# Recommender tower on one core: lookup groups of 8 to 10 blocks in a ring of 17, and gram products in runs of 64 samples

## What is computed

```python
    e = jnp.stack([tbl_0[ids[:, 0]], tbl_1[ids[:, 1]],
...
    gram = jnp.einsum('bfd,bgd->bfg', all_emb, all_emb)
    return gram[:, _TRIU_I, _TRIU_J]
...
    h = jnp.concatenate([z, r_bottom_output], axis=1)
    h = jnp.maximum(h @ W_top1 + b_top1, 0.0)
    h = jnp.maximum(h @ W_top2 + b_top2, 0.0)
    y = h @ W_top3
```

## Time and profile before

| | us |
|---|---|
| median of 3 runs (358.92 to 360.71) | 360.54 |
| span of the profiled execution | 357.7 |
| PE busy in it | 334.8 (94%) |
| DVE busy | 267.5 (75%) |
| POOL busy | 254.7 (71%) |
| ACT busy | 205.6 (57%) |

### The profile page before, as it was taken

One profiled execution on the slowest core, in us unless ns is written; L12 is line 12 of the kernel. 1 busy time (PEld: TensorE's weight loads), 2 busy tenths in 40 slices (PEclk: granted clock), 3 DMA queues, 4 the chain that ended last, 5 costly groups with the idle time before them and its releaser, 6 DMA issues.

```text
span 357.7 us, 14104 instructions
## 1 busy us (share of the span) xinstructions
PE 334.8 (94%) x6020; PEld 295.8 (83%) x6020; DVE 267.5 (75%) x810; ACT 205.6 (57%) x336; POOL 254.7 (71%) x274
## 2 busy tenths in 40 slices
PE   0678989899999999999999999999999999999996
PEld 0677889798988988888888888889888888888885
DVE  1999999994868869598777978788696987732412
ACT  3585776232334774757757566849666578552232
POOL 4777777777777777777777777777777777777600
DMA  6657468332225855849567496657766394732200
GB/s 211 180 166 244 136 172 295 96 83 63 55 53 112 150 113 106 131 101 176 101 129 131 84 151 134 127 104 121 155 99 141 85 175 109 106 83 57 58 5 1
DMA packets 60013, 42.91 MB, mean 120 GB/s; under 512 B 48816, under 2 KB 51504, under 8 KB 59824
## 3 DMA queue, kind: packets, MB, share of 16 engines
q1 hardware_dynamic: 51216, 24.38, 33.2%
q0 software_dynamic: 8448, 17.32, 20.9%
q10 hardware_dynamic: 288, 0.33, 0.4%
HBM read 31.24 MB, written 0.01 MB: 87 GB/s over the span
## 4 chain that ended last, share of the span: by engine, by line
PE 53%; DVE 16%; POOL 12%; DMA 9%; issue 5%; ACT 2%; SPq 2%; ACTq 0%; DVEq 0%
PE hot_ps L458 18%; POOL X L406 12%; DVE onehot L682 11%; PE h_ps L490 8%; PE gram_ps L436 8%; PE xt_ps L458 7%; PE h_ps L535 5%; DMA ids_wide<-in_hot_ids_dram 4%; PE h_ps L487 3%; DVE tab L749 2%; DMA stage_sb<-in_hot_dram 2%; DMA X<-in_table_dram,rows_sb 2%; PE xt_ps L420 1%; DMA turned<-planes 1%; PE zt_ps L472 1%
## 5 line engine op out<-in xcount | busy, mean ns | idle before, releaser
L406 POOL DMA_INDIRECT X<-in_table_dram,rows_sb x264 | 253.3, 959 | 83.3 <-issue 78.9
L682 DVE TENSOR_SCALAR onehot<-ids_wide,row_value 128x256 fp32r<-128x256 int16 x665 | 206.2, 380 | 39.2 <-PE hot_ps L458 23.2
L458 PE MATMUL hot_ps<-onehot,tab 128*128 128x256 f32 x1072 | 149.5, 291 | 14.4 <-ACT tab L861 11.1
L458 PEld LDWEIGHTS hot_ps<-onehot,tab 128*128 128x128 f32 x1072 | 135.2, 193 | 17.8 <-issue 15.3
L658 ACT COPY XT<-turned 128x512 int16<-128x512 int16 x82 | 65.7, 883 | 8.6 <-DMA turned<-planes 8.6
L832 ACT COPY XT<-hot_ps 128x256 f32<-128x256 f32 x60 | 41.2, 686 | 50.4 <-PE hot_ps L458 50.2
L436 PEld LDWEIGHTS gram_ps<-XT 128*27 128x27 f32 x4096 | 40.6, 105 | 28.3 <-issue 18.1
L436 PE MATMUL gram_ps<-XT 128*27 128x26 f32 x4096 | 53.0, 190 | 4.4 <-DVE Z L690 3.3
L822 ACT COPY planes<-X 128x1024 int16<-128x1024 int16 x41 | 44.5, 1086 | 13.2 <-DMA X<-in_table_dram,rows_sb 13.2
L490 PE MATMUL h_ps<-stage_sb,w_sb 128*128 128x256 f32 (+3 forms) x192 | 44.2, 366 | 0.0
L458 PE MATMUL xt_ps<-onehot,tab 128*128 128x256 f32 x288 | 40.8, 288 | 0.0
(11 more groups left out here) (54 smaller groups left out, 134.9 us busy)
## 6 DMA issues: line engine op xcount, KB each, us to landing
ids_wide<-in_hot_ids_dram SPq DMA_DIRECT2D x14, 320.0 KB, 4.6
X<-in_table_dram,rows_sb POOLq DMA_INDIRECT x264
stage_sb<-in_hot_dram SPq DMA_DIRECT2D x15, 256.0 KB
stage_sb<-in_hot_dram SPq DMA_DIRECT2D x10, 192.0 KB
bottomT<-in_bottom_t_dram SPq DMA_DIRECT2D x8, 128.0 KB
w_sb<-in_w_dram SPq DMA_DIRECT2D x1, 1024.0 KB
turned<-planes SPq DMA_TRANSPOSE x41
w_sb<-in_w_dram SPq DMA_DIRECT2D x1, 512.0 KB, 9.3
```

The costliest lines, as they stand in the source:

```text
L406: pool.indirect_dma_start(X[:, n % RING, k, :], None, table, bass.IndirectOffsetOnAxis(idx[:, column:column + 1], 0)).then_inc(gathered[n ...
L458: mm = pe.matmul(hot_bank(i)[:, 0:WIDE], tab[u][:, part, D * c:D * (c + 1)], onehot[p % ONEHOTS][:, c - PIECE[u][h], :], start=(c == 0 and ...
L682: compared = dve.tensor_scalar(onehot[p % ONEHOTS][:, c - PIECE[u][h], :], ids_wide[:, u, :], row_value[:, c:c + 1], None, ALU.is_equal)
```

## The change

**Groups.** The 64 blocks are cut into seven groups of 8, 9, 9, 10, 9, 10 and 9 blocks (`TAKEN`) instead of eight of 8. A lookup product has 32 columns for each block of its group, so 256, 288 or 320; each group after the first still has 180 products. The slices spread them over the blocks of the group before: 22 or 23 a block in blocks 0 to 7, 20 in groups of 9 blocks, 18 in groups of 10. No lookups are left from block 55 on.

**Ring.** XT is a ring of 17 blocks instead of 16, indexed by block. A copy that crosses the end of the ring is made as two (`kept`): all placings of groups 3 and 5 and some copies of outside vectors. Since a group may be longer than what is free, ScalarE holds back the placings of a group's first blocks until enough of the ring is free (`placed_in`), and places them together in the first block where it is.

**One-hots.** Pieces are now two chunks (`BITE`), in six buffers: 12 chunks instead of 20 places. Loading and splitting of the tables stays in pieces of up to 4 chunks (now 4 + 4 + 2 for 10).

**Order of tables.** From group 2 on (the third group) the tables are looked up in reverse, the five of 10 chunks first.

**Order on TensorE.** From block 16 to 53 (`TURN_FROM` to `LAST` - 2) two blocks are one step, `half_tile`: the lookups of both, the gram products of both, then the MLP steps of both.

The rest follows from these: narrower slices of the id lists, the waits of the lists by group, and the scratch of ScalarE's share of the comparisons, which moves into a buffer of the DMA transposes.

```diff
-XTILES = 4
-WIDE = 2 * P
+KEPT = 17
-ONEHOTS = 5
+ONEHOTS = 6
+BITE = 2
-GROUPS = TILES // 2
+TAKEN = [8, 9, 9, 10, 9, 10, 9]
+GROUPS = len(TAKEN)
+STARTS = [sum(TAKEN[:n]) for n in range(GROUPS + 1)]
+WIDE = PAD * max(TAKEN)
...
+ORDER = [list(range(HOTS[n])) if n < 2 else list(range(HOT))[::-1] for n in range(GROUPS)]
...
+        def placed_in(b):
+
+            early = STARTS[GROUP_OF[b] + 2] - KEPT if GROUP_OF[b] + 2 <= GROUPS else 0
+            if b < early:
+                return []
+            if b == early:
+                return [i for k in range(STARTS[GROUP_OF[b]], b + 1) for i in ended(k)]
+            return ended(b)
...
-                    mm = pe.matmul(hot_bank(i)[:, 0:WIDE], tab[u][:, part, D * c:D * (c + 1)],
-                                   onehot[p % ONEHOTS][:, c - PIECE[u][h], :],
+                    mm = pe.matmul(hot_bank(i)[:, 0:width(n)], tab[u][:, part, D * c:D * (c + 1)],
+                                   onehot[p % ONEHOTS][:, c - BITES[u][h], 0:width(n)],
...
+            def half_tile(b):
+
+                t, j = b // BLOCKS, b % BLOCKS
+                lookups(*slice_of(b))
+                lookups(*slice_of(b + 1))
+                gram(b)
+                gram(b + 1)
+                mlp(t, j)
+                mlp(t, j + 1)
...
-            for b in range(LAST - 1):
+            for b in range(TURN_FROM):
                 step(b)
+            for b in range(TURN_FROM, LAST - 2, 2):
+                half_tile(b)
+            step(LAST - 2)
             last_blocks()
...
-                wait(act, gram_full, 2 * BLOCKS * (n - 1))
-                act.copy(XT[:, at:at + 2, :, hot_slot(u)], hot_bank(i)[:, 0:WIDE].rearrange("d (t s) -> d t s", t=2)
-                         ).then_inc(hot_placed, 1)
+                wait(act, gram_full, STARTS[n + 1] - KEPT)
+                for begin, end, at in kept(STARTS[n], STARTS[n + 1]):
+                    columns = slice(PAD * (begin - STARTS[n]), PAD * (end - STARTS[n]))
+                    placed = act.copy(XT[:, at, :, hot_slot(u)],
+                                      hot_bank(i)[:, columns].rearrange("d (b s) -> d b s", s=PAD))
+                placed.then_inc(hot_placed, 1)
...
-                for i in ended(b)[:1]:
+                placed = placed_in(b)
+                for i in placed[:1]:
                     place_hot(i)
                 split_words(UNITS_OF.get(b + AHEAD, []))
                 for p in pieces_ended(b):
                     one_hot_share(p + ONEHOTS)
-                for i in ended(b)[1:]:
+                for i in placed[1:]:
                     place_hot(i)
```

More of the change, by code:

```diff
@@ L72, in hot_slot, with pieces, kept @@
     return BOTTOM_SLOT + 1 + u if u < HOT_BASE else ALWAYS + u - HOT_BASE
-def pieces(chunks):
-    count = -(-chunks // PIECE_MAX)
-    return [-(-chunks * h // count) for h in range(count + 1)]
+def pieces(chunks, most):
+    return list(range(0, chunks, most)) + [chunks]
+def kept(begin, end):
+    out = []
+    while begin < end:
+        stop = min(end, (begin // KEPT + 1) * KEPT)
+        out.append((begin, stop, slice(begin % KEPT, begin % KEPT + stop - begin)))
+        begin = stop
+    return out
 def pick(rows):
@@ L124, in build @@
     PER_STEP = -(-len(LATE_PIECES) // SPLIT_STEPS)
-    PRODUCTS = [[PARTS * sum(HC[:u]) for u in range(h + 1)] for h in HOTS]
-    SLICES = RUNS * BLOCKS * 2
+    PRODUCTS = [[PARTS * sum(HC[u] for u in order[:k]) for k in range(len(order) + 1)] for order in ORDER]
     with ExitStack() as ctx:
@@ L283, in is_last, with asked_of @@
             i, u, h = ASKED[p]
-            return h == len(PIECE[u]) - 2
+            return h == len(BITES[u]) - 2
+        def asked_of(q):
+            u, k = PIECE_OF[q]
+            return [ASKED_AT[u, h] for h in range(len(BITES[u]) - 1) if PIECE[u][k] <= BITES[u][h] < PIECE[u][k + 1]]
         def wait_bottom(eng, t):
@@ L838, in place_bottom @@
                     return
[L839 removed]
+                wait(act, gram_full, BLOCKS * (t + 1) - KEPT)
                 wait_bottom(act, t)
[L841 to L842 removed]
+                bottoms = bottomT[:, t % BOTTOMS, :].rearrange("d (q g) -> d g q", q=4)
+                for begin, end, at in kept(BLOCKS * t, BLOCKS * (t + 1)):
+                    rows = slice(PAD // 4 * (begin - BLOCKS * t), PAD // 4 * (end - BLOCKS * t))
+                    placed = act.copy(XT[:, at, :, BOTTOM_SLOT].rearrange("d b (g q) -> d (b g) q", q=4), bottoms[:, rows, :])
+                placed.then_inc(bottom_placed, 1)
             def relu(g, c):
@@ L985 @@
     starts = _np.tile(lists, (PAD, 1))
-    hot_ids = ids[sample][:, :, hot].reshape(GROUPS, WIDE, HOT).transpose(0, 2, 1).astype(_np.int16)
+    hot_ids = _np.zeros((GROUPS, HOT, WIDE), _np.int16)
+    blocks = ids[sample][:, :, hot].reshape(TILES * BLOCKS, PAD, HOT)
+    for n in range(GROUPS):
+        hot_ids[n, :HOTS[n], :PAD * TAKEN[n]] = blocks[STARTS[n]:STARTS[n + 1]].reshape(-1, HOT).T[ORDER[n]]
     feature = features(hot, rest)
```

159 lines of the change are left out of this document (83 added, 76 removed).

## The result

| | before | after |
|---|---|---|
| median of 18 runs each, us | 360.23 (358.92 to 364.63) | 357.25 (355.57 to 359.10) |
| ratio of the times, 95% interval | | 0.9916 [0.9893, 0.9939] |
| span of the profiled execution (time of that execution of after: 355.85) | 357.7 | 354.1 |

The change makes the kernel 0.8% faster: 3.0 us by the medians, 3.6 us by the two profiled spans. The time lies inside the range, but one term of the sum had the wrong sign, and the number came out near for other reasons.

A forecast was written before the change was run, and what follows sets the result against it. TensorE bounds the kernel, with GpSimd's gathers close behind. TensorE's terms bring blocks 16 to 55 from 204.2 to 192.2 us, below the gathers' 195.4, so the gathers set span 353.3: median 356.1 us, range 353.5 to 360.5.

The forecast's parts named there:

- The two bounds: TensorE (5.24 us a block) and GpSimd's gathers (5.01) nearly tie; TensorE's savings count only until the gathers are reached.
- My 353.3 for the tail: Span if TensorE waits for the last gather, 4.4 us below 357.7; TensorE must gain 4.5 us before block 55.
- Lookups: TensorE, blocks 16 to 55: products of 288 and 320 columns at 0.130 and 0.140 us gain 8.2 us.
- 64 strips in a row: TensorE, blocks 16 to 53: 57 fewer runs of gram products, each with a fixed price, save 14 us.
- ScalarE's handshake (+6.7): In pairs, TensorE waits for ScalarE's move before the second block's gram: 0.35 us in 19 pairs, 6.7 us lost.
- VectorE (+3.5): Fewer one-hot chunks ahead and wider comparisons fall just short: some 0.7 us, 5 times, 3.5 us lost.
- The sum: TensorE, blocks 16 to 55: 204.2 - 8.2 - 14 + 6.7 + 3.5 = 192.2 us; gathers 195.4.
- rival A: Waits eat part of TensorE's gain, with late first blocks on top: median 358 to 360; chance 0.18.
- B: Slower: a pair's loop closes through ScalarE's moves, over 1.0 us a pair, 19 us: 366; chance 0.10.
- C: Better: the gathers come sooner, winning back 4 us of slack: span 349.3, median 352; chance 0.07.
- The first 16 blocks: VectorE is full there; wider comparisons against fewer chunks ahead: +0.5 us of lead at block 16, bounds -2 and +3.
- the signs that I named: Last gather at 338 +- 1, transposes within 2.5 us; ScalarE's gather waits over 30; gram 14 us less.

The follow-up runs named there:

- experiment 3: The changed kernel with the MLP step of a pair's first block between the two blocks' gram products (runs of 64 records): 357.4 us, ratio 0.9872.
- Experiment 1: The changed kernel with every block a step of its own, without pairs and long runs (groups alone): 356.25 us, ratio 0.9863.
- experiment 2: The kernel before with only the pairs of blocks from block 16 to 53, lookups still 256 wide: 369.26 us, ratio 1.021.
- experiments 4: The changed kernel without pairs, with each block's gram products in one run of 64 from block 16 on: 356.06 us, ratio 0.9862.
- experiment 5: The changed kernel with its pairs, but a pair's gram products in four runs of 32 records: 356.52 us, ratio 0.988.
- Experiment 6: The changed kernel without pairs and with eight groups of 8 blocks, all else of the change kept: 361.38 us, ratio 1.0013.
- early list: The changed kernel without pairs, plus a small buffer loading the second group's first three tables of ids early: 357.25 us, ratio 0.9881.
- groups again: The changed kernel block by block, without pairs, timed a second time: 356.63 us, ratio 0.9888.

## Why the prediction was near, and what in it was wrong

**The two bounds: right.** The gathers are as they were, 1.25 us each. No profiled execution with all gathers has a span under 354.1 us, and of all their executions the shortest span is 353.0; with a fourth of the gathers left out the profiled spans are 352.7, 351.7 and 349.7. My 353.3 for the tail was 0.8 below what after reached in its profile: the last gather came 0.5 later than in the trace before, the rest is what TensorE was behind. What I missed is that the gathers already bind at block 57's transposes (experiment 3).

**Lookups: right in kind, the pitch mis-sized.** Two streams of after:

```profile
187.02 2.79 PE L498 MATMUL xt_ps<-onehot,tab 128*128 128x288 f32 x20
```

With 0.30 us for the last, (2.79 - 0.30) / 19 = 0.131 us, by the starts 0.133; the 320-wide one at 218.42 above gives (3.10 - 0.31) / 19 = 0.147. I had 0.130 and 0.140. 256, 288 and 320 columns at 0.120, 0.133 and 0.147 are one column per 0.416 ns, the 2.4 GHz clock, and 0.013 us. So columns set the pitch from 256 on, and my argument from the 0.127 us of the transposes was no evidence. In the streams that is 108.0 - (380 x 0.133 + 360 x 0.147) = 4.5 us instead of 8.2. Experiment 1 shows 7.2 us of lookup time less; 2.7 of it lie outside the streams' pitch, and 1.9 of these are waits of before (1.7 for VectorE's `Z`, 0.2 for a move) between the last lookup and the gram products, which the groups alone don't have. The formula that the Trainium skill gives for an isolated product (N/2.4 + 2.5 ns, "TensorE: Matmul & The Clock Gate", "Back-to-back issue gap") has the slope that this case's traces show and a constant 10 ns too small for these products.

**64 strips in a row: the step that failed.** I had -14 us for 57 runs fewer: 0.19 us of edge each (10.8), and 3.2 for the inside of the runs, read from a run of 64 records and carried on to 128. The edges gave some 7 (lookups 3.1, MLP and the rest 4.1), 0.13 each. The inside, which I took to be straight beyond 64 records, cost 10.0 more, all of it in the holes. The trace of before held a warning that I passed by: among its nine runs of 64 two take 0.73 and 0.80 us instead of 0.67. Experiments 2 to 5 agree: pairs with runs of 32 bring nothing (TensorE 1.4 us longer than with the groups alone), runs of 64 save TensorE 2.3 and 3.7 us, and runs of 128 raise the gram time by 10.0 us in after and by 13.1 with the pairs alone (1.9 of it waits for moves).

What slows the records behind the 32nd, and what makes the holes, is not settled. The load's idle time is put down to "issue", which names no cause, and nearly all holes lie inside one block's gram products, where the program has no wait; the one exception is in the next paragraph. The Trainium skill ("TensorE: Matmul & The Clock Gate", "Architectural detail: the array is 16× 32×32, not 1× 128×128") gives TensorE a queue of 64 instructions; 32 loads and 32 products are 64, and this case's trace agrees so far as the pace changes there. That instructions come in more slowly than such short ones run would explain both pace and holes, but no run here tests it. The trace only shows that holes don't need a transfer on the instruction DMA queue close by: three of the 19 runs have none in them or in the 1.5 us before, and have two or three holes each.

**ScalarE's handshake (+6.7) and VectorE (+3.5): over-sized.** TensorE's waits in after, us in total, times, longest:

```profile
PE hot_ps L498 <- DVE onehot L731: 13.8, 10, 10.4
PE h_ps L575 <- DVE h L788: 2.1, 4, 0.5
```

Of the 13.8 us 10.4 are the start; in all products of 288 and 320 columns it is 0.9. Between 110 and 320 us it waits for a move of ScalarE once, 0.5 us: the gram products of block 19 start at 128.53, and the move of block 19 ended at 128.48, though the profile puts the wait down to "issue". The kernel of experiment 5, whose runs are short, has no such wait; pairs alone wait 1.9 us and the changed kernel, profiled again, once for 2.5. I had reckoned 0.35 in every one of 19 pairs; it happens in none to two of them. The second row is a wait that I had put at nothing: with two MLP steps back to back the second tile's second layer waits for VectorE to take the first's result, four times 0.5 us. Before has none of it, and it is why the second layer costs more in the table above.

**The sum.** -8.2 - 14 + 6.7 + 3.5 = -12.0 predicted, -4.4 measured. The tail needed 4.5 us of gain to meet the gathers. With 12 it would have waited for them, with 4.4 it just got there, and the end of the profiled execution is the same within 1 us: the floor of the gathers forgave an error of 7.6 us. That is luck, and there is more of it. The profiled execution is one of the fastest of after: the median span of its 18 is 355.5 us, 2.2 above my 353.3. But I had added 2.8 us of time outside the span, and in after it is 1.7 to 1.8 in every execution (in the executions of before beside the experiments, 1.7 to 3.5). So of the 3.0 us that the medians gained some 0.7 to 0.9 lie outside the span, where I had reckoned no gain. Experiment 6 has 1.7 to 1.8 too and experiment 2 1.8 to 3.2, so neither the width nor the pairs bring it; what does is open. In the profile the outcome is the edge between the forecast and rival A, reached on another path. B is out (waits for moves of 0.5 to 2.5 us, not 17), and so is C: the gathers' lost time rose from 3.7 to 5.2 us. The first 16 blocks were right: the end of block 15's gram products moved by 0.15 us. Of the signs that I named, the last gather (338.45) and the transposes behind it came as forecast; ScalarE's waits for gathers rose from 13.2 to 17.5 us and not over 30, and the gram time rose where it was to fall by 14.

## What to carry to other kernels

When two engines are within a few per cent of each other, reckon first what the second allows; a gain on the first counts only up to there, and a wait at that point may cost the clock as well. Look for every place where the first engine needs the second, not only the last one: here block 57's transposes met the gathers before the tail did. Don't merge short products into longer runs on the strength of a fixed cost read from short runs: read the pace of the late records in the longest run there is, and look for holes in it. And time the parts of a change alone: here the groups alone gave 1.1 and 1.4%, at least as much as the whole, and pairs with runs of 128 alone cost the old kernel 2%.

## What the runs showed of the hardware

- Products with 27 weights and 26 columns start every 7.5 ns for 32 records (0.35 us a run up to the next product) and some 9 ns apart behind them, with holes of mostly 0.2 to 0.3 us: 0.67 us at best and 0.77 and 0.79 on average for 64 (experiments 4 and 3), 1.23 at best and 1.93 on average in after for 128.
- Wide products in a stream: 0.120, 0.133 and 0.147 us for 256, 288 and 320 columns.
- After 1.66 us (groups alone, experiment 1) and 2.1 us (experiment 3) in which TensorE had nothing to do, the granted clock was 0.68 and 0.50 in the stretches behind, and the work there took up to 1.7 times as long (transposes 1.12 us instead of 0.66). The length of the pause alone doesn't tell: after pauses of 3.23 and 3.10 us (experiments 3 and 4, just before block 55) it stayed at 1.00, and the transposes took 0.63.
- A gather's data came 1.4 to 1.7 us after its record's end at block 57 in after and in experiments 1 and 5, and 2.4 to 2.7 us after it in the four traces where TensorE waited for them (experiments 3 and 4, early list, groups again); in before it was 3.6.
